# An attention block on one core: the products of a single key block as one fp32 matmul each, with other places for some steps

## The reference

```python
h = layernorm(x) * (1 + ca) + sa                    # sa, ca, ga, ... from silu(c) @ wmod
q = h @ wq   # 32 heads of 128;   k, v = h @ wk, h @ wv   # 8 heads of 128
q, k = rope(q), rope(k)                             # x*cos + rotate_half(x)*sin
att = softmax(where(causal, q @ k.T / sqrt(128), -inf))
x = x + ga * ((att @ v) @ wo)                       # 4 query heads share one k, v head
h = layernorm(x) * (1 + cb) + sb
x = x + gb * (h @ W.T + b + router_lora(h))         # one of 4 ranks kept per row
```

## Time and profile before

| | |
|---|---|
| profiled execution | 1064.88 us, span of the instructions 1063.1 us |
| TensorE | busy 1038.9 us (98%), 5426 matmul records |
| VectorE | 786.1 us (74%) |
| ScalarE | 634.5 us (60%) |
| GpSimd | 528.6 us (50%) |
| granted TensorE clock, mean | 0.997 |

### The profile page before, as it was taken

One profiled execution on the slowest core, in us unless ns is written; L12 is line 12 of the kernel. 1 busy time (PEld: TensorE's weight loads), 2 busy tenths in 40 slices (PEclk: granted clock), 3 DMA queues, 4 the chain that ended last, 5 costly groups with the idle time before them and its releaser, 6 DMA issues.

```text
span 1063.1 us, 16548 instructions
## 1 busy us (share of the span) xinstructions
PE 1038.9 (98%) x5426; PEld 867.4 (82%) x5426; DVE 786.1 (74%) x1834; ACT 634.5 (60%) x1294; POOL 528.6 (50%) x510
## 2 busy tenths in 40 slices
PE   6999999999999999999999999999999999999997
PEld 3678888888888888888888888888888888887875
DVE  5688875787668875688758876688758875687666
ACT  5457763587447764477437764488436754477433
POOL 4536562466336563365435654365535653364334
PEclk9999999999999999999999999999999999999999
DMA  8363323223402323123302233133312233032001
GB/s 303 105 200 96 106 58 80 66 75 90 109 1 74 111 75 80 60 81 90 85 25 70 90 100 80 36 94 95 89 26 71 80 89 100 34 96 71 1 21 60
DMA packets 98285, 86.92 MB, mean 82 GB/s; under 512 B 39380, under 2 KB 84052, under 8 KB 98072
## 3 DMA queue, kind: packets, MB, share of 16 engines
q1 hardware_dynamic: 97384, 85.75, 27.5%
q10 hardware_dynamic: 816, 0.10, 0.1%
HBM read 59.23 MB, written 26.61 MB: 81 GB/s over the span
## 4 chain that ended last, share of the span: by engine, by line
PE 76%; DVE 7%; issue 6%; ACT 6%; POOL 5%; DMA 0%; POOLq 0%; DVEq 0%
PE accumulators L694 17%; PE accumulators L709 17%; PE accumulators L675 16%; PE scores L625 13%; PE transposed L638 7%; PE scores L899 2%; ACT p_large L934 2%; POOL qc L1639 2%; DVE pb_lo L1251 2%; POOL p_small L1622 1%; PE accumulators L732 1%; POOL p_large L1622 1%; ACT qr L967 1%; ACT qr L966 1%; DVE p_small L1239 1%
## 5 line engine op out<-in xcount | busy, mean ns | idle before, releaser
L1622 POOL TENSOR_SCALAR p_large<-p_large,rowinv 128x640 f32<-128x640 f32 (+3 forms) x128 | 127.9, 999 | 205.5 <-DVE rowinv L1244 205.5
L942 ACT ACTIVATE pb_hi<-transposed 128x512 fp32r<-128x512 f32 (+3 forms) x256 | 120.9, 511 | 137.1 <-PE transposed L638 136.7
L1631 POOL TENSOR_TENSOR qr<-qr,trig 128x512 f32<-128x512 f32 x80 | 103.7, 1296 | 187.3 <-ACT qr L967 187.3
L1251 DVE TENSOR_TENSOR pb_lo<-transposed,pb_hi 128x512 fp32r<-128x512 f32 (+3 forms) x256 | 141.4, 583 | 47.6 <-ACT pb_hi L942 46.5
L934 ACT ACTIVATE p_large<-p_large,negmax 128x640 f32<-128x640 f32 (+3 forms) x128 | 126.4, 987 | 83.2 <-DVE negmax L1239 81.7
L1239 DVE CUSTOM_DVE_ANT_0 p_large<-scores,mask 128x640 f32<-128x640 f32 (+3 forms) x128 | 129.6, 1016 | 14.1 <-PE scores L625 9.0
L625 PE MATMUL scores<-k_hi,q_hi 128*128 128x512 f32 (+2 forms) x384 | 139.6, 364 | 0.0
L1622 POOL TENSOR_SCALAR p_small<-p_small,rowinv 128x128 f32<-128x128 f32 (+3 forms) x128 | 96.8, 772 | 80.7 <-DVE rowinv L1244 80.7
L625 PE MATMUL scores<-k_hi,q_lo 128*128 128x512 f32 (+2 forms) x384 | 132.0, 344 | 0.0
L625 PE MATMUL scores<-k_lo,q_hi 128*128 128x512 f32 (+2 forms) x384 | 131.3, 342 | 0.0
L1639 POOL TENSOR_TENSOR qc<-qc,qr 128x512 f32<-128x512 f32 x80 | 121.4, 1517 | 5.6
(11 more groups left out here) (181 smaller groups left out, 2245.9 us busy)
## 6 DMA issues: line engine op xcount, KB each, us to landing
p_rows<-turned SPq DMA_DIRECT2D x31, 640.0 KB, 2.9
pa_lo<-p_rows SPq DMA_DIRECT2D x124, 160.0 KB, 3.1
stage<-in_L_attn_wq_dram SPq DMA_DIRECT2D x32, 256.0 KB, 2.8
stage<-in_L_attn_wo_dram SPq DMA_DIRECT2D x32, 256.0 KB, 3.5
v_rows<-vt SPq DMA_DIRECT2D x32, 128.0 KB, 2.7
v_lo<-v_rows SPq DMA_DIRECT2D x32, 128.0 KB, 3.2
y<-in_L_wmod_dram SPq DMA_DIRECT2D x4, 512.0 KB, 6.9
stage<-in_L_attn_wk_dram SPq DMA_DIRECT2D x8, 256.0 KB, 2.7
```

The costliest lines, as they stand in the source:

```text
L942: nc.scalar.activation(pt_of(i, part, True), src, ACT.Copy).then_inc(t_hi, 1)
L1251: nc.vector.tensor_tensor(pt_of(i, part, False), src, f32(pt_of(i, part, True)), ALU.subtract).then_inc(t_lo, 1)
L1622: nc.gpsimd.tensor_scalar(row(i), row(i), rowinv[:, i:i + 1], 1.0, ALU.mult, ALU.mult).then_inc(s_norm, 1)
L1631: nc.gpsimd.tensor_tensor(qr[:, s, :], qr[:, s, :], trig[:, 1, half * HALF:(half + 1) * HALF], ALU.mult).then_inc(r_sin, 1)
```

## The change

The products of a single block become one fp32 matmul of 128 columns each. Score tile 0 takes `k_first` (a copy of the first 128 keys) and the unsplit rotated q; the last key block of the early product takes `v_third` (a copy of the v block) and the unsplit block that lies in `pa_lo`; that of the late product takes the unsplit v block and `late_corner`, a new copy by VectorE. What was split only for them is no longer split, and the zero blocks go. Beside that, instructions move: VectorE's and ScalarE's steps in heads 2 and 3, GpSimd's last normalisation in head 3, the silu columns of the first group from VectorE to ScalarE, VectorE's steps at the start of the last group, and in the FFN the last `kept_ranks` and the last addition.

```diff
-        PIECES = {0: [256], 1: [256], 2: [384], 3: [512], 4: [384, 256], 5: [512, 256], 6: [512, 384], 7: [512, 512]}
+        PIECES = {0: [], 1: [256], 2: [384], 3: [512], 4: [384, 256], 5: [512, 256], 6: [512, 384], 7: [512, 512]}
...
             js = parts(i)[part]
-            n = len(js)
+            n = len(js) - (js[-1] == NT - 1)
...
+
+        early_corner = pa_lo[:, :, 10, :]
...
                 key = 0
+                if i == 0:
+                    query = q_first[:] if h == 0 else qc[:, N.slot("r", ("q", (h, 0)), at), 0:P]
+                    mm = nc.tensor.matmul(S_flat[:, c0:c0 + P], query, k_first[:], start=True, stop=True)
                 for n in PIECES[i]:
...
+                single = 4 * half + 3
                 for done, count, products, keys in steps:
                     pe.wait_ge(done, count)
                     for v, hi in products:
                         for j in keys:
-                            c0, pt = pt_row(j, half, hi)
-                            mm = nc.tensor.matmul(acc[:, c0:HALF], v[:, j, :], pt, start=(hi and v is v_hi and j == 0),
-                                                  stop=(not hi and j == 4 * half + 3))
+                            if j < single:
+                                c0, pt = pt_row(j, half, hi)
+                                nc.tensor.matmul(acc[:, c0:HALF], v[:, j, :], pt, start=(hi and v is v_hi and j == 0), stop=False)
+                if half == 0:
+                    corner = q_first[:] if n > LAST else f32(early_corner)
+                    mm = nc.tensor.matmul(acc[:, 3 * P:HALF], v_third[:], corner, start=False, stop=True)
+                else:
+                    mm = nc.tensor.matmul(acc[:, 3 * P:HALF], f32(v_lo[:, NT - 1, :]), late_corner[:], start=False, stop=True)
                 mm.then_inc(a_full, 1)
...
             transposes(3, 5, G7)
+            scores(3, 7, G7)
             weight_transposes(3)
-            scores(3, 7, G7)
...
-                if t >= 1:
+                if 1 <= t < NT:
...
+                if t == NT - 1:
+                    kept_ranks(t)
...
-                nc.scalar.activation(pa_blocks(pa_hi), f32(pa_blocks(pa_lo)), ACT.Copy).then_inc(pa_hi_done, 1)
+                nc.scalar.activation(pa_blocks(pa_hi, 10), f32(pa_blocks(pa_lo, 10)), ACT.Copy).then_inc(pa_hi_done, 1)
...
-                nc.scalar.activation(v_hi[:], f32(v_lo[:]), ACT.Copy).then_inc(v_hi_done, 1)
+                nc.scalar.activation(v_third[:], f32(v_lo[:, 3, :]), ACT.Copy)
+                nc.scalar.activation(v_hi[:, 0:NT - 1, :], f32(v_lo[:, 0:NT - 1, :]), ACT.Copy).then_inc(v_hi_done, 1)
...
+                if half == 0 and (kind == "k" or which[0] == 0):
+                    single = k_first if kind == "k" else q_first
+                    nc.scalar.activation(single[:], qc[:, N.slot("r", name, at, ahead), 0:P], ACT.Copy)
...
+                if at.first and not h:
+                    act.wait_ge(a_full, N.value("a", ("mod", "second"), at))
+                    for k in range(KC):
+                        ins = nc.scalar.activation(vt[:, k * P:(k + 1) * P], ident[:], ACT.Identity,
+                                                   bias=silu[:, 3, k:k + 1], scale=0.0)
+                    ins.then_inc(silu_done, 1)
...
-                exp(h, 7, at)
                 if last:
                     fill(h, 5, at, slice(0, 1))
+                exp(h, 7, at)
...
+                if j < 3:
+                    nc.scalar.activation(pa_row(pa_hi, j), row_bank(j), ACT.Copy).then_inc(t_hi, 1)
+                else:
+                    nc.scalar.activation(q_first[:], TB[:, N.slot("t", ("e", 3), G7), 0:P], ACT.Copy).then_inc(t_hi, 1)
...
+                    n = len(js) - (js[-1] == NT - 1)
+                    bank = TB[:, N.slot("t", name, at, ahead), :]
+                    src = bank[:, 0:n * P].rearrange("p (a b) -> p a b", b=P)
+                    if n < len(js):
+                        nc.vector.tensor_copy(late_corner[:], bank[:, n * P:HALF])
...
-                        if which == "second":
...
-                            for k in range(KC):
-                                ins = nc.vector.tensor_scalar(vt[:, k * P:(k + 1) * P], mask[:, 0:P],
-                                                              silu[:, 3, k:k + 1], None, ALU.add)
-                            ins.then_inc(silu_done, 1)
...
+                tail = head_number(h, at) == LAST
                 if h:
                     masked(h, 4, at)
+                if h and not tail:
                     masked(h, 5, at)
                     inverse(h, 4, at)
...
-                masked(h, 7, at)
-                transposed_lo(h, 5, at)
                 if h == 2:
+                    transposed_lo(h, 5, at)
+                    masked(h, 7, at)
                     early_lo(h, at)
+                else:
+                    masked(h, 7, at)
+                    transposed_lo(h, 5, at)
...
+                if last:
+                    fill(h, 5, at, slice(0, 1))
                 inverse(h, 7, at)
                 if last:
-                    fill(h, 5, at, slice(0, 2))
+                    fill(h, 5, at, slice(1, 2))
...
+                if j < 3:
+                    nc.vector.tensor_tensor(pa_row(pa_lo, j), row_bank(j), f32(pa_row(pa_hi, j)), ALU.subtract).then_inc(t_lo, 1)
+                else:
+                    nc.vector.engine_nop().then_inc(t_lo, 1)
 
             early_row_lo(0)
             early_row_lo(1)
+            inverse(3, 4, G7)
+            masked(3, 5, G7)
...
+            masked(3, 7, G7)
             weight_lo(("W", 3), 4, fw_hi[:, 3, :], fw_lo[:, 3, :])
-            masked(3, 7, G7)
...
+                if t == NT - 1:
+                    kept_ranks_lo(t)
...
+            dve.wait_ge(f_gated, NT)
+            dve.wait_ge(f_y, NT)
+            dve.wait_ge(f_out, NT - 1)
+            nc.vector.tensor_tensor(y[:, NT - 1, :], y[:, NT - 1, :], f_tmp((NT - 1) % 2), ALU.add).then_inc(f_out, 1)
...
+                if last:
+                    rotate(("k", 0), at, 1)
                 normalise(h, 7, at)
                 if last:
-                    rotate(("k", 0), at, 1)
...
-            for pad in (pa_hi[:, :, 0, :], pa_lo[:, :, 0, :], pb_hi[:, 27, :], pb_lo[:, 27, :]):
-                nc.gpsimd.memset(f32(pad), 0.0)
```

More of the change, by code:

```diff
@@ L300, in adaln_block @@
         turned = sb("turned", [P, 10 * P])
-        pb_hi, pb_lo = sb("pb_hi", [P, 29, P], F32R), sb("pb_lo", [P, 29, P], F32R)
+        pb_hi, pb_lo = sb("pb_hi", [P, 26, P], F32R), sb("pb_lo", [P, 26, P], F32R)
         o_hi, o_lo = sb("o_hi", [P, R, T], F32R), sb("o_lo", [P, R, T], F32R)
@@ L314, in adaln_block @@
         vt = sb("vt", [P, T])
+        late_corner = sb("late_corner", [P, P])
+        q_first, k_first, v_third = sb("q_first", [P, P]), sb("k_first", [P, P]), sb("v_third", [P, HD])
         p_small = sb("p_small", [P, 1280])
@@ L421, in turned_blocks, with pa_blocks @@
             return rows[:, :, at:at + step * (len(js) - 1) + 1:step, :].rearrange("p b j r -> p j b r")
-        def pa_blocks(buf):
-            return buf[:, :, 1:11, :].rearrange("p a l r -> p a (l r)")
+        def pa_blocks(buf, last=11):
+            return buf[:, :, 1:last, :].rearrange("p a l r -> p a (l r)")
         def pa_row(buf, j):
@@ L1138, in early_row_hi @@
                 act.wait_ge(t_full, N.value("t", ("e", j), G7))
-                nc.scalar.activation(pa_row(pa_hi, j), row_bank(j), ACT.Copy).then_inc(t_hi, 1)
+                if j < 3:
+                    nc.scalar.activation(pa_row(pa_hi, j), row_bank(j), ACT.Copy).then_inc(t_hi, 1)
+                else:
+                    nc.scalar.activation(q_first[:], TB[:, N.slot("t", ("e", 3), G7), 0:P], ACT.Copy).then_inc(t_hi, 1)
             early_row_hi(0)
@@ L1269, in early_lo @@
                 dve.wait_ge(pa_hi_done, n + 1)
-                nc.vector.tensor_tensor(pa_blocks(pa_lo), f32(pa_blocks(pa_lo)), f32(pa_blocks(pa_hi)),
+                nc.vector.tensor_tensor(pa_blocks(pa_lo, 10), f32(pa_blocks(pa_lo, 10)), f32(pa_blocks(pa_hi, 10)),
                                         ALU.subtract).then_inc(pa_lo_done, 1)
@@ L1517, in early_row_lo @@
                 dve.wait_ge(t_hi, N.value("t", ("e", j), G7))
-                nc.vector.tensor_tensor(pa_row(pa_lo, j), row_bank(j), f32(pa_row(pa_hi, j)), ALU.subtract).then_inc(t_lo, 1)
+                if j < 3:
+                    nc.vector.tensor_tensor(pa_row(pa_lo, j), row_bank(j), f32(pa_row(pa_hi, j)), ALU.subtract).then_inc(t_lo, 1)
+                else:
+                    nc.vector.engine_nop().then_inc(t_lo, 1)
             early_row_lo(0)
             early_row_lo(1)
+            inverse(3, 4, G7)
+            masked(3, 5, G7)
             weight_lo(("W", 0), 1, fw_hi[:, 0, :], fw_lo[:, 0, :])
```

11 lines of the change are left out of this document (6 added, 5 removed).

## The result

The changed kernel takes 1053.43 us (median of 4 runs, 1051.72 to 1053.55) against 1064.78 for the kernel before on the same chip (4 runs): ratio 0.9891, 95% interval 0.9878 to 0.9905, 11.35 us less. The forecast was 1050.5, range 1044.5 to 1058.5: the sign and the range hold, and 3 us of the forecast gain of 14.3 are missing. The profiled execution took 1053.54 us, its span is 1051.8.

What follows compares the result with a forecast made beforehand. TensorE was taken as the limit in one half of each group, the chain through ScalarE, VectorE and GpSimd in the other. Gains of 6.3 (products), 2.7 (orders) and 5.5 us (ends) from 1064.88 gave 1050.5, range 1044.5 to 1058.5.

Steps and rivals of the forecast that it cites:

- The single products: Three one-block products per head: 0.215 us each as fp32 instead of 0.36, 0.255 gained per head after going back.
- The price of going back: On TensorE, the first split matmuls after an fp32 run were said to cost 0.09 us more.
- Rival 4: Fp32 products bound by weights loaded anew each pass, 0.44 us each: slower, +5.2 us, about 1070; chance 0.04.
- Rival 1: Going back to split matmuls costs nothing, 0.435 us gained per head: 1046 us; chance 0.20.
- What of it reaches the end: Products' net gain per group: 0.455 us in the TensorE half, 0.33 in the chain half, 6.3 over 8 groups.
- I cost them at nothing: ScalarE's new copies of `q_first`, `k_first`, `v_third`, about 0.28 us each, said to lie where ScalarE waits: cost nothing.
- The wait for `qc`, 2.7 us: Moved orders in head 3 remove TensorE's 0.39 us wait before the value projection, 7 groups: 2.7 us.
- Head 2's order, nothing: `pb_lo` of tile 5 before tile 7's mask removes one wait, but the next transposes wait for GpSimd: no gain.
- The start, 0.9: First group: silu columns moved from VectorE to ScalarE remove the wait before TensorE's transposes: 0.9 us.
- The very end, 1.3: FFN end: rank transposes before tile 6's low-rank product and last addition on VectorE gain 1.3 us.
- The last group, 3.3 us: `pa_lo` before tile 5's mask removes TensorE's stop (1.9 us) and the half clock after it (1.7); 3.3 taken.
- Rival 3: Last group's stop stays, changes only its releaser, and the clock falls again: 3.6 us less gain, 1054; chance 0.09.

Runs made afterwards that it cites:

- e3: Changed kernel with score tile 0 and the early product's last block as split matmuls again, the late product still fp32: 1058.96 us, ratio 0.9946.
- e4: Changed kernel plus one more fp32 product of 128 columns in each head, between score tiles 1 and 2: 1055.99 us, ratio 0.9924.
- e6: Changed kernel with VectorE's old order in head 2 (mask of row 7 before the low parts of tile 5): 1051.95 us, ratio 0.9892.
- e1: Changed kernel with every moved order put back, only the three fp32 products and their copies kept: 1059.11 us, ratio 0.9949.
- e9: Kernel of e5 with ScalarE's copy of `q_first` moved behind the swap of the next key's halves: 1052.60 us, ratio 0.9891.
- e2: Kernel before with the moved orders alone, all products still split matmuls: 1061.38 us, ratio 0.9969.
- e5: Changed kernel with the old order in head 3 put back on ScalarE, VectorE and GpSimd: 1055.41 us, ratio 0.9921.
- e7: Changed kernel with ScalarE's swap for the second value projection put ahead of `pa_hi` in head 3: 1049.35 us, ratio 0.9863.
- e8: Changed kernel, last group: tile-6 transposes before tile 0's output projection, last FFN weight's low part before row 7's mask: 1050.37 us, ratio 0.9876.
- e10: Changed kernel with VectorE's copy of the late product's corner moved behind the reciprocals of rows 0 to 2: 1052.24 us, ratio 0.9883.
- e11: Changed kernel with the edits of e7, e8 and e10 together: 1046.60 us, ratio 0.9836.

## Why the prediction came out as it did

**TensorE's limit in one half of the group, the chain in the other: right.** The stretches of the first half shrink by what the products save, those of heads 2 and 3 don't, and e3, e4 and e6 show it from three sides.

**The single products: mechanism right, one term wrong.** The price of one product, 0.215, was right (0.22). The price of going back, 0.09, doesn't exist. It was read from the length of the first split record behind the router, 1.17 instead of 1.08; but such a record starts early while the fp32 pass before it still runs, and the starts of the next ones show no gap. I read a duration where only steps between starts could tell. Rival 4 (0.44 a product) is out for this shape. The estimate from the four passes that the Trainium skill names (FP8 and Floating Point Precision, section TensorE Precision Notes) was 0.24 a product, near the 0.22. The estimate from the load price in the Trainium skill's TensorE: Matmul & The Clock Gate, section LDWEIGHTS (loading the stationary operand), taken once for each of four passes, was 0.43, twice what is measured. The trace has one load for each record (x5330 of PE and of PEld in the busy row), so two a product and not four. Rival 1 had the TensorE time right (0.435 a head, measured 0.415), yet not the end: it gave 1046.

**What of it reaches the end: too little here, too much there.** The first half of the group gives 0.69 (forecast 0.455 for the pairs and the late product in it). The second half was forecast at 0.33 and gives 0.26, although each product saves more: the row for T4(2) already sets TensorE's time there (in e4 a product added ahead of it costs nothing by then), and the copy of the corner and the chain add 0.16 at T4(3).

**"I cost them at nothing": wrong for `q_first`.** This step failed. The forecast put the copy into a stretch in which ScalarE waits, but in head 3 ScalarE has no gap from that copy to the swap (e1). With the old order the copy costs 0.22 a group (e1, e9); with the new order it is hidden.

**The wait for `qc`, 2.7 us: wrong.** The term took the 0.39 at the first value projection as gone. ScalarE's exponential and `pa_hi` now stand ahead of the swap for the second one, and the wait is there: alone the order gives nothing (e2). Its worth of 0.40 a group beside the products (e5) is mostly cover for what the products bring. The forecast said that the exponential's later end is hidden and never asked what is queued behind it.

**Head 2's order, nothing: right** (e6).

**The start, 0.9: right** (1.1). **The very end, 1.3: 0.9.** VectorE's last addition waits for GpSimd's of tile 6, as foreseen; but that one comes 0.2 to 0.3 us later than assumed, since the low-rank product of tile 6 now stands behind the rank transposes, and 0.14 passes before VectorE starts.

**The last group, 3.3 us: wrong.** The step "with the stop gone" failed: the stop moved, both traces have the lower clock behind it, and 0.5 us is won (e2). Rival 3, given 0.09, has it: the stop changes its releaser. I looked for it at the early rows, it stood at the output projection, since the same change moved the mask of row 7 ahead of the bank's release. That move is in the diff and got no sentence of its own. The 1.7 us for the clock were besides no fixed price of a stop: e6, e7 and e9 keep the stop and don't pay them.

By terms: products and orders in the groups 6.3 + 2.7 = 9.0 forecast, about 8.2 measured (8 x 1.02); start 0.9 against 1.1; last group's stop 3.3 against 0.5; end 1.3 against 0.9; and two that nobody forecast, 0.86 of one group of before and -0.58 of the beginning. That the total fits better than its terms is luck: an undervalued product stands against an overvalued order.

## What to carry to other kernels

When a wait is taken from one place, follow the engine that had made it and ask what now stands ahead of its next release; here one wait only changed projection and another only changed bank. Read the price of a matmul from the steps between starts, behind it too, never from the length of one record. Time parts both alone and together: these were worth 6.7 and 3.1 us apart and 11.9 together in the traces past the beginning, since one covered what the other cost. And before a loss is put down to an order, look whether other executions with the same order have it.

## What the runs showed of the hardware

**GpSimd and VectorE hold each other up.** At the beginning VectorE normalises the last tile of x. In the changed kernel's trace the operations ahead of it came 0.7 us later than in e8, and it started while GpSimd was subtracting `wk_lo` (19.20 to 20.47): 1.45 us. In e8 it started before that: 0.72. The changed kernel, then e8:

```profile
19.30 1.45 DVE L1510 TENSOR_SCALAR p_large<-p_large,rstd,shift 128x512 f32<-128x512 f32 x1
```

```profile
18.63 0.72 DVE L1510 TENSOR_SCALAR p_large<-p_large,rstd,shift 128x512 f32<-128x512 f32 x1
```

That goes with the two beginnings: in the four traces that reach the value projection at 35.1 to 35.3 us (the changed kernel, e3, e5, e10) the operation takes 1.27 to 1.63 us and ends 0.28 behind GpSimd's subtraction; in the nine at 34.2 to 34.6 it takes 0.54 to 0.75. The Trainium skill, SBUF — State Buffer, section Who interferes with whom, says that VectorE, in its modes that use two ports, and GpSimd share a port pair, and that whoever issues first holds it for the whole instruction while the other is blocked. These four endings agree with that; no run here shows the ports themselves. In the long group of before, and in the same group of e2, GpSimd's row 4 starts within 0.02 us of VectorE's `wk_lo`, and TensorE waits 1.0 us for it.

**Behind the same stop the clock falls in some executions and not in others.** Eleven of the thirteen traces have a stop of about 2 us in the last group (1.94 to 2.12 shown). In eight of them the granted clock behind it falls to the lower level, 1.2 GHz, and in the changed kernel that costs 1.6 us more. In three (e6, e7, e9) it stays at 1.00. The runs of the changed kernel fit this: three with a mean clock of 0.997 took 1053.3 to 1053.6 us, the one with 0.999 took 1051.72. A short stop is no sure sign either: e11, without such a stop, has the clock at 0.50 from 20 to 22 us, behind 4 us in which TensorE was busy all the time, and still reaches the value projection at 34.3. What decides it no run here shows.
